# A decoder stack of five attentions: turning the exponentials of softmax on VectorE and by DMA instead of on TensorE

## The reference

```python
x = L0(x, ctx)   # 16-head cross attention; its result for sequence 0 is added to every sequence
x = L1(x, ctx)   # Mamba-2 block (conv of 4 taps, silu, 8 heads, state 128), then 8-head cross attention with padding mask
x = L2(x, ctx)   # 16-head causal self attention, 16-head cross attention, layernorms, a 256-256-256 MLP, zero-row masks
x = L3(x, ctx)   # 16-head causal cross attention + residual, layernorm, 256-1024-256 MLP with exact gelu
# in each attention:
probs = softmax(q @ k.T * scale); att = probs @ v
```

## Time and profile before

| | |
|---|---|
| median of three runs | 1736.97 us (1736.25 to 1737.17) |
| profiled execution, span from first to last instruction | 1734.3 us, mean granted TensorE clock 0.988 |
| PE / PEld busy | 96% / 83% of the span |
| ACT / DVE / POOL busy | 78% / 76% / 31% |
| DMA | 26.92 MB, mean 16 GB/s |
| chain that ended last | PE 88%, DVE 7%, issue 2% |

### The profile page before, as it was taken

How to read it: one execution, slowest core, us unless ns; L and a number is a source line. 1 busy time by engine, 2 the same in 40 slices (tenths; PEclk the granted TensorE clock), 3 DMA queues, 4 the chain that set the end, 5 groups by cost and what they waited for, 6 DMA issues and landing times.

```text
span 1734.3 us, 54906 instructions
## 1 busy us (share of the span) xinstructions
PE 1664.1 (96%) x21232; PEld 1438.0 (83%) x21232; DVE 1313.4 (76%) x3355; ACT 1357.1 (78%) x4026; POOL 533.5 (31%) x1288
## 2 busy tenths in 40 slices
PE   6789999999999999999999999999999999999976
PEld 6577888888888888888888888888888888888765
DVE  3577778887778888877888887788888778888542
ACT  2367888888888888888888888888888888888763
POOL 1333233332323333232333333233333323333110
PEclk9899999999999999999999999999999999999998
DMA  7000000000000000000000000000000000000000
GB/s 266 8 8 8 8 8 12 6 10 9 11 12 11 11 6 10 9 11 11 12 11 8 8 8 11 12 11 11 10 5 9 10 11 11 9 5 5 5 4 10
DMA packets 26176, 26.92 MB, mean 16 GB/s; under 512 B 2240, under 2 KB 25024, under 8 KB 25792
## 3 DMA queue, kind: packets, MB, share of 16 engines
q1 hardware_dynamic: 25920, 23.41, 4.1%
HBM read 19.21 MB, written 4.19 MB: 13 GB/s over the span
## 4 chain that ended last, share of the span: by engine, by line
PE 88%; DVE 7%; issue 2%; ACT 1%; POOL 1%; DMA 0%; DVEq 0%; SPq 0%; POOLq 0%; ACTq 0%
PE ring L581 26%; PE ring L587 22%; PE ring L569 18%; PE score L637 6%; PE ring L678 5%; PE ring L755 3%; PE ring L765 2%; DVE conv L1237 2%; PE ring L668 2%; PE ring L816 1%; DVE conv L1231 1%; PE score L628 1%; DVE neg_max L1144 1%; PE ring L748 1%; ACT exps L954 1%
## 5 line engine op out<-in xcount | busy, mean ns | idle before, releaser
L954 ACT ACTIVATE exps<-score,neg_max 128x128 f32<-128x128 f32 x1808 | 491.4, 409 | 112.7 <-DVE neg_max L1144 112.7
L1144 DVE TENSOR_REDUCE neg_max<-score 128x4 f32<-128x512 f32 x452 | 289.8, 683 | 118.9 <-PE score L637 118.8
L1400 POOL TENSOR_TENSOR stat<-stat 128x1 f32<-128x1 f32 x224 | 128.8, 575 | 698.3 <-DVE stat L1116 698.3
L960 ACT COPY weights<-ring 128x512 f32<-128x512 f32 x452 | 257.3, 658 | 44.0 <-PE ring L569 42.3
L569 PE MATMUL ring<-const,exps 128*128 128x128 f32 x1808 | 240.1, 275 | 11.6 <-ACT exps L954 7.9
L569 PEld LDWEIGHTS ring<-const,exps 128*128 128x128 f32 x1808 | 210.2, 142 | 33.9 <-ACT exps L954 15.8
L1231 DVE SCALAR_TENSOR_TENSOR conv<-raw,vectors,conv 128x128 f32<-128x128 f32 x576 | 168.5, 348 | 6.8
L581 PE MATMUL ring<-actT,w_q 128*128 128x128 f32 x1024 | 138.0, 278 | 2.5 <-ACT actT L926 2.5
L637 PE MATMUL score<-K,QB 32*128 32x128 f32 x3616 | 135.2, 283 | 0.5 <-issue 0.5
L637 PEld LDWEIGHTS score<-K,QB 32*128 32x128 f32 x3616 | 113.8, 188 | 21.9 <-issue 21.7
L926 ACT COPY actT<-ring 128x256 f32<-128x256 f32 x224 | 86.4, 386 | 56.3 <-PE ring L569 56.3
(11 more groups left out here) (165 smaller groups left out, 3472.5 us busy)
## 6 DMA issues: line engine op xcount, KB each, us to landing
cT<-in_ctxT SPq DMA_DIRECT2D x32, 128.0 KB, 2.1
x_in<-in_x SPq DMA_DIRECT2D x32, 128.0 KB, 2.0
out<-result SPq DMA_DIRECT2D x32, 128.0 KB, 2.1
row_all<-in_rows SPq DMA_DIRECT2D x1, 1420.0 KB, 10.2
w_in<-in_in_proj SPq DMA_DIRECT2D x1, 1288.0 KB, 7.2
w_k<-in_k SPq DMA_DIRECT2D x4, 256.0 KB, 6.1
w_v<-in_v SPq DMA_DIRECT2D x4, 256.0 KB, 6.3
w_q<-in_q SPq DMA_DIRECT2D x4, 256.0 KB, 6.8
```

Of the source, the lines that this page charges most:

```text
L954: last = run(exps[:, n, h * P:(h + 1) * P], of, ACT.Exp, bias=neg_max[:, m, h:h + 1])
L960: nc.scalar.copy(weights[:, buffer(it, a_, l, t, WEIGHT_BUFFERS), half * 4 * P:(half + 1) * 4 * P], t_[:, :]).then_inc(read, 1)
L1144: nc.vector.tensor_reduce(neg_max[:, m, 4 * half:4 * half + 4].rearrange("p (b h) -> p b h", b=each), score[:, first:first + each, 0:4 // ...
L1400: tt(stat[:, l, 10:11], stat[:, l, 2:3], stat[:, l, 4:5], ALU.pow).then_inc(S[done], 1)
```

## The change

- Parts of attentions 0 to 3 (five of a sequence's seven): `turn` and `turned_out` go. DVE transposes the whole part in place in blocks of 32 x 32 (`turn_blocks`), and SP issues four DMAs from SBUF to SBUF (`move_blocks`), each from 32 partitions of `exps` to all 128 of `weights`, 128 KB in runs of 1 KB. Attention 4's two parts stay with PE and ACT (`BY_PE`).
- Keys now stand in the order 4i + b. So K2 (ACT, two instructions instead of one), K1, K3, K4, the row mask and the masks are written in blocks from strided reads, and ACT writes a streamed part in runs of 32 elements; attention 4's exponentials are written with a stride of four elements, so that they are in order of the keys' new numbers.
- `exps` has three buffers instead of two, and ACT waits for the landing of the DMAs of the part three before. K1 and V1 have two lanes instead of four.
- Attention 1's sums: each of its eight exponentials gets an accumulator output; DVE takes the reciprocal of 128 x 8; eight PE matmuls with `ident` spread it (as many as those with `ones` before), ACT copies the 128 x 256 output, DVE multiplies.
- From DVE to ACT: the first tap of the convolution (six instructions a sequence), `xhat`, both zero-row tests (Abs with accumulator). From DVE to POOL: `x1`, the second product of `gate`, the affine step of all seven roots, the comparisons of the tests.
- All of `TASKS`, `FIRST`, `LAST`, `SETUP` and `SHIFT` is new. Places on PE, before to after: quads1 9.7 to 11.7, values1 12.1 to 15.8; quads2 15.3 to 19.1, values2 19.8 to 24.0; quads3 25.9 to 28.7, values3 27.6 to 32.4; quads4 34.0 to 37.9, values4 39.7 to 43.5; xhatT -8.8 to -5.2, down 68.3 to 56.9. On SP the order within a period of 14 is now turn3_1, turn2_0, turn2_1, store, loadc, loadx, turn1_0, turn3_0.

```diff
+BY_PE = ((4, 0), (4, 1))
-EXPS_BUFFERS = 2
+EXPS_BUFFERS = 3
-RING_JOBS.update({f"turn{a_}_{t}": f"turn{a_}_{t}0 turn{a_}_{t}1" for a_ in PARTS for t in range(PARTS[a_])})
+RING_JOBS.update({f"turn{a_}_{t}": f"turn{a_}_{t}0 turn{a_}_{t}1" for a_, t in BY_PE})
...
+            def move_blocks(it, a_, l, t):
+                n, _ = turned(it, a_, l, t)
+                part_of = exps[:, buffer(it, a_, l, t, EXPS_BUFFERS), :]
+                sp.wait_ge(S["flipped"], flipped(it, a_, l, t))
+                old = slot_before(it, a_, l, t, WEIGHT_BUFFERS)
+                if old is not None:
+                    was_a, _, was_l, was_i = old
+                    b, use = job(Of(was_i), f"values{was_a}", was_l)
+                    sp.wait_ge(bank_read[b], use + 1)
+                for q, rows_of in enumerate(ROWS_OF):
+                    sp.dma_start(weights[:, n, q * 2 * P:(q + 1) * 2 * P],
+                                 part_of[rows_of].rearrange("i (b x) -> i b x", b=TILES)).then_inc(S[f"turned{n}"], 16)
...
-                evacuated_all(it, *V_job, *[j for t in range(PARTS[a_]) for j in turn_jobs(a_, l, t)], then=(f"values{a_}", l))
+                evacuated_all(it, *V_job, *[j for t in by_pe for j in turn_jobs(a_, l, t)], then=(f"values{a_}", l))
+                for t in range(PARTS[a_]):
+                    if t not in by_pe:
+                        n, count = turned(it, a_, l, t)
+                        pe.wait_ge(S[f"turned{n}"], count)
...
+                into = exps[:, n, :].rearrange("p (h i b) -> p h b i", h=HEADS, b=TILES) if (a_, t) in BY_PE else exps[
+                    :, n, :].rearrange("p (b h i) -> p h b i", b=TILES, h=HEADS)
+                old = slot_before(it, a_, l, t, EXPS_BUFFERS)
+                if old in STREAMED:
+                    was_a, was_t, was_l, was_i = old
+                    moved, count = turned(Of(was_i), was_a, was_l, was_t)
+                    act.wait_ge(S[f"turned{moved}"], count)
...
-                        last = run(exps[:, n, h * P:(h + 1) * P], of, ACT.Exp, bias=neg_max[:, m, h:h + 1])
+                        if a_ == 1:
+                            last = run(into[:, h], by_block(of), ACT.Exp, bias=neg_max[:, m, h:h + 1], accum_out=sums[:, l % 2, h:h + 1])
+                        else:
+                            last = run(into[:, h], by_block(of), ACT.Exp, bias=neg_max[:, m, h:h + 1])
...
+                for k in range(n):
+                    c = half * n + k
+                    last = run(conv[:, l % 2, c, :], t[:, k * P:(k + 1) * P], ACT.Identity,
+                               scale=conv_w[:, c, TAPS - 1:TAPS], bias=conv_b[:, c:c + 1])
+                last.then_inc(read, 1)
...
+            def turn_blocks(it, a_, l, t):
+                part_of = exps[:, buffer(it, a_, l, t, EXPS_BUFFERS), :]
+                dve.wait_ge(S["exps"], (part(it, a_, l, t) + 1) * HALVES)
+                nc.vector.transpose(part_of, part_of).then_inc(S["flipped"], 1)
+                if a_ == 1:
+                    nc.vector.reciprocal(shares[:, l % 2, :], sums[:, l % 2, :]).then_inc(S["shares"], 1)
...
-            def root(it, l, seed, done):
+            def root(it, l, step, seed, done, src=1, scale=1.0, offset=EPS):
                 wait_for(S[seed], nth(it, l))
+                step(ts(stat[:, l, 2:3], stat[:, l, src:src + 1], scale, offset, ALU.mult, ALU.add))
                 tt(stat[:, l, 10:11], stat[:, l, 2:3], stat[:, l, 4:5], ALU.pow).then_inc(S[done], 1)
```

More of the change, by code:

```diff
@@ L50 @@
 TASKS = dict(
[L51 to L58, removed]
@@ new lines @@
+    norm3=-10.4585, x4T=32.9635, fc1=33.8441, fc2=34.6456, norm4=54.9533, K4=35.8361, V4=38.4636, x5T=36.2148, Q4=37.2832,
+    finish4=47.6543, norm5=36.2044, x6T=45.6661, up0=46.6359, up1=46.7074, down=56.8897, store=89.3984, quads1=11.6814,
+    scores1_0=15.2308, turn1_0=18.7914, values1=15.768, quads2=19.1117, scores2_0=34.9423, scores2_1=44.8019, turn2_0=-33.4011,
+    turn2_1=42.7786, values2=23.9792, attT2=-31.2242, back2=25.0719, quads3=28.7133, scores3_0=-10.6879, scores3_1=32.0217,
+    turn3_0=13.1234, turn3_1=45.5657, values3=32.3969, attT3=26.6484, back3=32.5473, quads4=37.8683, scores4_0=12.9657,
@@ L315 @@
 in_time(NEXT_BUT_ONE, 2)
+for engine, one, other, later in ON_ENGINE:
+    for n in range(B - later):
+        m = n + later
+        assert PLACE_OF[engine][one, n % G, n // G] < PLACE_OF[engine][other, m % G, m // G], (engine, one, other, n)
 def before(keys, n, by, task, other):
@@ L1028, in Q1, with nonzero_rows, x2T, x3T @@
                 last.then_inc(read, 1)
+            def nonzero_rows(it, what, l, mask, done):
+                act.wait_ge(bank_full[job(it, what, l)[0]], job(it, what, l)[1] + 1)
+                run(att[:, l, :], res[:, l, :], ACT.Abs, accum_out=mask[:, l, 0:1]).then_inc(S[done], 1)
+            def x2T(it, l):
+                copy_out(it, "x2T", l, actT[:, l], D)
+                nonzero_rows(it, "x2T", l, mask0, "sum0")
+            def x3T(it, l):
+                copy_out(it, "x3T", l, actT[:, l], D)
+                nonzero_rows(it, "x3T", l, mask1, "sum1")
             def Q2(it, l):
                 query(it, "Q2", l)
+            def keys_out(it, what, lane):
+                t, read = filled(it, what, lane)
+                for c in range(DC):
+                    last = nc.scalar.copy(by_block(K2[:, lane, c, :]), in_blocks(t[:, c * P:(c + 1) * P]))
+                last.then_inc(read, 1)
             def K_2(it, l):
-                copy_out(it, "K2", l, K2[:, l], D)
+                keys_out(it, "K2", l)
             def V_2(it, l):
```

498 lines of the change are left out of this document (303 added, 195 removed), and 2 rows, old and new, of the table S.

## The result

| | before | after |
|---|---|---|
| median of four runs, us (lowest to highest) | 1736.77 (1736.25 to 1737.17) | **1872.64** (1866.81 to 1875.45) |
| ratio, 95% interval | 1 | 1.0775 [1.0755, 1.0796] |
| span of the profiled execution, us | 1734.3 | 1873.0 |

7.8% slower, 136 us, where 1611 us was forecast. That kernel took 1736.8 to 1739.4 us there, and a difference of two medians from different chips carries up to 3 us of this.

What follows compares the result with a forecast made beforehand. PE alone was taken as the bound: 1734.3 us, less 158.8 for removed turns, plus 4 at the start, gives 1579.5; 29 us of waits make 1608, and 2.7 from span to median 1611 us, range 1580 to 1645.

Steps and rivals of the forecast that it cites:

- PE is the bound and the next engine has 8.5 us of air: Level stretch: PE alone bounds the 50.51 us sequence; ACT, next at 42.0 us, leaves 8.5 us for the change.
- 1734.3 - 158.8: Whole run: profiled span less 162 turns removed from PE at 0.98 us each, all counted as time saved.
- The low end: ACT's strided exponential writes: no extra cost, leaving ACT at 42.3 us a sequence.
- my high end: ACT's strided exponentials in attention 4: the streaming part doubles, 1.6 us more a sequence.
- Covered by the 24 us that POOL has left: Small work moved to POOL: adds 4.5 us a sequence, 21.0 in all, and fits in POOL's free time.
- I take this as hidden, because PE works on other sequences meanwhile: Layernorm roots on POOL: each comes some 0.25 us later at no cost; uncovered, 1.8 us a sequence.
- The 2% of idle time: PE's waits because engines' fixed task lists do not mesh: 0.9 us a sequence, 29 us in all.
- The parts land late: Rival: PE waits for DMA landings at values of attentions 1 to 3, 3 us each; 1868 us, chance 0.09.
- ACT: Rival: strided writes and accumulators make ACT the bound at 45.0 us a sequence; 1672 us, chance 0.17.
- DVE: Rival: block transposes on VectorE take 2.45 us each, DVE reaches 45.5 us a sequence; 1656 us, chance 0.06.
- full house: Rival: PE keeps its 99.6% busy and the run's end shortens too; 1565 to 1575 us, chance 0.06.
- It does nothing: Rival: the new order costs what the saved turns bring; within 3.5 us of 1737, chance 0.02.

Runs made afterwards that it cites:

- run 10: Kernel before with the turns of five parts a sequence (attentions 1, 2, 3) left out, nothing in their place: 1732.38 us, ratio 0.9962.
- Runs 9: Kernel before with the turns of two parts a sequence (first of attentions 2 and 4) left out, nothing in their place: 1726.42 us, ratio 0.9924.
- runs 8: Changed kernel with the affine steps of five layernorms and the gate's second product back on VectorE: 1848.89 us, ratio 1.0651.
- 17: Changed kernel with its five transposes and their DMAs left out, affine steps and gate's second product back on VectorE: 1774.01 us, ratio 1.0205.
- run 12: Changed kernel with its five VectorE transposes and their DMAs left out: 1795.99 us, ratio 1.0318.
- run 15: Kernel before with two parts turned by VectorE and DMA, and the convolution's first tap moved to ScalarE: 1859.61 us, ratio 1.0692.

## Why the prediction was wrong

**The step that failed** is the first and largest: "PE is the bound and the next engine has 8.5 us of air", and with it "1734.3 - 158.8" in the sum. PE did lose its work (run 10: 4 us a sequence of the 4.9; a turn's 0.98 was taken too high, the chain of before has the same one at 0.87), and the time stayed. PE busy 199.2 of 200 us was read as: nothing else is as long. It only says that PE was never short of work. Runs 9 and 10 show a second bound at 50.0 to 50.2 us a sequence, made of dependences and of the order in which DVE and ACT take their tasks, beside which ACT and DVE have only 0.738 x 50.23 = 37 and 41 us of work. So of 159 us the two sets of turns that were left out brought 13 and 7 in that order, and the 8.5 us of air were no measure, since they are a mean: the stretch in which a transpose of attention 2 stands had 0.3 us.

**The 136 us**, by the runs: the new order with its small work, turns for nothing, is 1796 - 1737 = 59; VectorE's transposes add 1831 - 1796 = 35; the DMA leg adds 41.5. By the ratios, each against its own chip, the three are 55, 38 and 41. Cut the other way, the undisturbed sequence accounts for 32 x 2.88 = 92 us, of which new order 31, transposes 39, DMA leg 22. The other 44 are the stretches at the lower clock (some 1.4 us each in this kernel), single slower sequences, and the start and the end; for the clock the sum had no term.

Term by term:
- *ACT.* Predicted 42.3 a sequence, measured 0.765 x 54.15 = 41.4. The strided exponentials take 429.9 / 1552 = 0.277 us where the earlier trace rows gave 0.272. The low end held. The Trainium skill's rule on 16-byte lines (SBUF — State Buffer, section Door 1: The DMA port swizzle), which I weighed, would have wanted 1.6 us more by my high end; attention 4's strided exponentials show none of it, they follow each other at 0.254 us, the streamed ones at 0.249 to 0.252. Attention 1's with their accumulators follow at 0.344, where I had put 0.272 + 0.219. The taps were under-sized, 75.0 / 192 = 0.39 for 0.314, and hit nothing.
- *DVE.* The transpose is 1.242 us for my 1.23. DVE's amount, 0.782 x 54.15 = 42.3, is 3.0 over the 39.3: three taps of the convolution take 459 ns where they took 348, (233.3 - 168.5) / 32 = 2.0 us, and L1305 takes 715 for 485, 0.9 us. This is the missed term behind the step "Covered by the 24 us that POOL has left". POOL had the time, but some of its instructions slow VectorE's two-input operations beside them. "I take this as hidden, because PE works on other sequences meanwhile" fell with it: with the affine steps and the product back on VectorE, runs 8 and 17 take 22 to 24 us back.
- *SP and the DMAs.* An issue is 0.605 for 0.47, a landing 2.7 for 2.0, the leg some 5 for 3.5. By the places the cover should have been 12 to 16 us. It held for most parts: PE waits for landings 49 times, 46 us in all. The load on the DMA engines was under-sized, 93312 packets and 20% of their time for the 82944 and 13%, and bound nothing.
- *The 2% of idle time* that stood for lists that don't mesh was the right worry at a fifth of its size: PE waits 11% in the middle.

**The rivals.** "The parts land late" gave 1868, 5 us from the result, and was given 0.09. Its mechanism is there, but it was to cost 9 us a sequence at three waits; measured, the leg is worth 41.5 / 32 = 1.3. The number agrees by chance. *ACT*, *DVE* by slow transposes and *full house* did not happen. *It does nothing* came nearest in kind, "the order as a whole costs what the turns save"; it costs more. What was missing is a rival in which PE is full and not the only bound. The view that would have shown it was at hand: for each stretch in which PE runs without a wait, follow the other engines' chain between the same two ends, 11.2 of 11.5 us, instead of their busy share.

**What was to show it.** PE over 97% and ACT over 90% in the middle: 89% and 77%. 512 transposes on PE from exps and 1.2 us a block transpose: right. The signs of "wrong" fit only in part: PE is under 95%, but ACT isn't near 100%, and waits on the DMA of weights are a small share.

**What stays open.** Of the 59 us with the turns free, 22 are the affine steps and the gate's product. The other 37 are not in the undisturbed sequence, which is 50.5 us in both orders, but in the sequences with a lower clock, in single others that are slower, and in the start and the end. No run shows why the clock falls in one sequence and not in the next, which has the same waits of PE, or how much of the rest belongs to the order and how much to the moves that I didn't undo (x1 and xhat, the row tests, attention 1's reciprocals). Since the tap gains 53 us in one order and costs 28 or more in the other, a move's price outside its own order says little about it inside. No version that beats the kernel before was found: with turns for nothing the old order gained 13 us at best.

## What to carry to other kernels

A full engine isn't the bound alone when its order is written around waits: leave the work out first, put nothing in its place, and look at what is gained, before building its replacement. Here that kernel says 7 us where the ledger says 157. Price an added instruction by the chain at the place where it must stand, not by the engine's idle share, and take an order and the work that it was found for as one thing. And when TensorE begins to wait, compare sequences at the same granted clock first: part of the loss can be the clock's.

## What the runs showed of the hardware

- POOL can hold VectorE up. In the changed kernel's timeline (start, length, instruction):

```profile
923.25 1.31 POOL L1636 TENSOR_TENSOR zs<-tz,zs 128x512 f32<-128x512 f32 x1
923.48 1.37 DVE L1305 SCALAR_TENSOR_TENSOR res<-att,stat,row_all 128x256 f32<-128x256 f32 x1
```

POOL's product ends at 924.56, VectorE's instruction, 0.49 us elsewhere, at 924.85: 0.3 us later: most of its work was done only when POOL was through. All 128 of these instructions took 0.485 us in the kernel before; here the 30 that overlap this product took 1.37 on average, those with no POOL instruction beside them 0.485. In the same way nine taps of the convolution took 4.69 us, for 2.70 in the kernel before, while two of POOL's instructions ran:

```profile
956.72 4.69 DVE L1394 SCALAR_TENSOR_TENSOR conv<-raw,vectors,conv 128x128 f32<-128x128 f32 x9
...
957.67 1.51 POOL L1589 TENSOR_SCALAR tz<-tz 128x512 f32<-128x512 f32 x1 [1.45 <-ACT tz L1158]
959.26 1.27 POOL L1590 TENSOR_TENSOR zs<-tz,zs 128x512 f32<-128x512 f32 x1
```

The Trainium skill, SBUF — State Buffer, section Who interferes with whom, has this rule: a VectorE instruction with two inputs in SBUF contends with a GpSimd instruction that reads SBUF, the shared port pair is an exclusive lock, and the order of issue decides who blocks. The trace agrees, 1.37 us for 0.49 for the one that issued second. It speaks against this change and should have been a term of it.
- A block transpose of 128 x 1024 in float32 takes 1242 ns, about what the product over a tile of that width took before (L1266, 1226 ns). The Trainium skill's 311 ns for 128 x 128 in bf16 (VectorE: DVE Perf Modes, section The three transpose paths) would make an estimated 2.5 us of it; here it takes half.
- An issue of 128 KB from SBUF to SBUF holds SP for 0.605 us (median, 1.95 at most) and it lands after 2.7 (5.5 at most).
- The granted clock. In the kernel before, where PE hardly waited, it was 1.00 in the middle. With PE waiting 11% of the time it was 0.98, from short stretches at the lower level, 1.2 GHz. In run 12's two windows above PE waits 1.76 us for VectorE in both sequences, and after it eight matmuls of w_q take 1.07 us in the first and 1.67 in the second, eight of w_out 1.99 and 2.98; the second sequence is 1.6 us longer. In run 15 it is 1.8, in the changed kernel 1.3 to 1.5.
